# Three PSUM banks in turn, and logits relative to the first tap's

## The reference

```
k = conv(x, w1, 7x7, dilation 2, pad 6) + b1      # 256 -> 128 channels
k = conv(k, w2, 1x1) + b2                         # 128 -> 49 logits a pixel
attn = softmax(k over the 49)
x = sum over the 49 taps of shifted(x) * attn
```

## Time and profile before

| what | us |
|---|---|
| median of 3 runs (1031.37 to 1032.67) | 1032.48 |
| the profiled execution | 1033.16 |
| its span, first to last instruction | 1031.4 |
| PE busy | 870.8 (84%) |
| PE weight loads busy | 815.1 (79%) |
| DVE busy | 670.4 (65%) |
| ACT busy | 378.2 (37%) |
| POOL busy | 321.5 (31%) |
| mean granted TensorE clock, of full speed | 0.94 |

### The profile page before, as it was taken

The page is one execution under the profiler, slowest core; times in us unless marked ns, Lnnn a source line. Parts: engine busy times, 40 slices in busy tenths (PEclk is TensorE's granted clock), DMA queues, the critical chain, the costliest instruction groups (busy, mean ns, idle before and its releaser), DMA issues.

```text
span 1031.4 us, 13805 instructions
## 1 busy us (share of the span) xinstructions
PE 870.8 (84%) x5084; PEld 815.1 (79%) x5084; DVE 670.4 (65%) x913; ACT 378.2 (37%) x647; POOL 321.5 (31%) x257
## 2 busy tenths in 40 slices
PE   5548969898998998999899899899667649969992
PEld 5548969898998998999899799899656537758882
DVE  1765677567778678676667767855544455139994
ACT  1222211243333433344344243333333466133267
POOL 2536455263255245227224524422200000004000
PEclk9999989999999999999899999999867869989997
DMA  9600224966775794885577576464687977000099
GB/s 287 211 0 1 42 53 104 204 176 149 166 194 133 172 202 114 207 178 163 156 173 180 146 174 151 124 188 109 177 206 194 209 269 296 1 1 1 26 388 401
DMA packets 261851, 163.11 MB, mean 158 GB/s; under 512 B 203817, under 2 KB 244762, under 8 KB 259226
## 3 DMA queue, kind: packets, MB, share of 16 engines
q1 hardware_dynamic: 261786, 162.24, 58.7%
HBM read 103.41 MB, written 53.97 MB: 153 GB/s over the span
## 4 chain that ended last, share of the span: by engine, by line
PE 49%; DVE 26%; DMA 8%; issue 7%; ACT 5%; POOL 2%; SPq 2%; DVEq 0%; ACTq 0%; POOLq 0%
PE ps L782 13%; PE ps L783 13%; PE ps L784 13%; DVE logit L1156 4%; DVE logit L1147 4%; DVE whole L1063 3%; PE ps L848 3%; DVE xbuf L1083 3%; DMA dn<-logit 3%; PE ps L888 3%; PE ps L805 2%; ACT y L774 2%; PE ps L858 2%; DMA out<-y 2%; DVE wsum L1036 2%
## 5 line engine op out<-in xcount | busy, mean ns | idle before, releaser
L782 PE MATMUL ps<-w_hi,ring 128*128 128x350 f32 x832 | 282.5, 340 | 12.1 <-DVE logit L1147 11.4
L784 PE MATMUL ps<-w_hi,ring 128*128 128x350 f32 x832 | 273.9, 329 | 0.0
L783 PE MATMUL ps<-w_lo,ring 128*128 128x350 f32 x832 | 273.5, 329 | 0.0
L551 POOL TENSOR_TENSOR ring<-whole,ring 128x576 fp32r<-128x576 f32 x112 | 168.2, 1503 | 263.5 <-ACT ring L618 263.5
L782 PEld LDWEIGHTS ps<-w_hi,ring 128*128 128x128 f32 x832 | 162.2, 195 | 13.4 <-issue 12.8
L783 PEld LDWEIGHTS ps<-w_lo,ring 128*128 128x128 f32 x832 | 161.8, 194 | 0.5
L784 PEld LDWEIGHTS ps<-w_hi,ring 128*128 128x128 f32 x832 | 160.9, 193 | 0.0
L618 ACT ACTIVATE ring<-whole 128x576 fp32r<-128x576 f32 x112 | 86.4, 775 | 142.3 <-DVE whole L1063 100.2
L618 ACT ACTIVATE band_hi<-ps 128x320 fp32r<-128x320 f32 (+1 forms) x128 | 53.6, 419 | 190.9 <-PE ps L848 190.7
L782 PE MATMUL ps<-band_hi,xT_hi 128*128 128x224 f32 (+2 forms) x320 | 99.2, 310 | 17.0 <-DVE x_lo L1000 10.0
L1000 DVE TENSOR_TENSOR band_lo<-ps,band_hi 128x320 fp32r<-128x320 f32 (+1 forms) x128 | 58.8, 459 | 72.5 <-ACT band_hi L618 72.4
(11 more groups left out here) (127 smaller groups left out, 1435.2 us busy)
## 6 DMA issues: line engine op xcount, KB each, us to landing
xq<-in_x SPq DMA_DIRECT2D x128, 256.0 KB, 4.0
raw<-bands SPq DMA_DIRECT2D x32, 768.0 KB, 5.5
xbuf<-in_x SPq DMA_DIRECT2D x16, 1024.0 KB, 8.5
x_dram<-x SPq DMA_DIRECT2D x32, 512.0 KB, 2.8
x1in<-x_dram SPq DMA_DIRECT2D x8, 2048.0 KB, 17.0
out<-y SPq DMA_DIRECT2D x16, 1024.0 KB, 4.5
bands<-wide SPq DMA_DIRECT2D x32, 398.0 KB, 5.5
w1raw<-in_L_conv_w SPq DMA_DIRECT2D x2, 3136.0 KB, 12.6
```

The source lines that it names most:

```text
L551: pool.tensor_tensor(split(k, 1), positions(whole[:, k % TBUFS, :], 0, 2), split(k, 0).bitcast(F32), ALU.subtract).then_inc(sig_lo_done, 1)
L782: pe.matmul(dst, l_hi, r_hi_, start=first, stop=False, **kw)
L783: pe.matmul(dst, l_hi, r_lo_, start=False, stop=False, **kw)
L784: return pe.matmul(dst, l_lo, r_hi_, start=False, stop=last, **kw)
```

## The change: what it does

- **48 columns.** `KP` is 48. The filter and the bias of tap 0 are subtracted from those of the other 48 (`w2T`, `b2row`), so the logits are relative to tap 0's, whose own is 0. The softmax takes the maximum with 0 and writes its negative as the entry of tap 0. All convolution matmuls have 336 columns instead of 350.
- **Combination.** The bias is laid out as 480 columns once and enters with the first step. ACT takes the HALF1 product out of its bank (`half_product`); DVE adds MHALF to it and subtracts it (`C_EVEN`, `C_ODD`), and four steps read only SBUF. 15 DVE steps a pair instead of 18, at other places of the half.
- **Softmax.** Normalising and masking are one pass over the probabilities instead of two, with a small product ahead of it.
- **Banks.** `band_T`, `x_T` and `proj` take the banks 5, 6 and 7 in turn (`turns`, `take_bank`), each when the one three turns before has been read. The prologue's filter groups take four banks in turn (`psW`).
- **x_lo.** `x1_lo` is made by POOL from `x1` (SBUF) instead of by DVE from PSUM, as long as the convolution runs; in halves 16 to 19 DVE makes it, from `x1` too. The first unit of a half image waits for the copy alone.
- **c_of** is four instructions of 576 columns, each of which waits for the one before.
- **Order.** The spill is issued before the x1 store. In each engine's half the steps are placed anew: `softmax_top` in part 4, `softmax_end` and `y_out(tail, 1)` in part 7, `proj(tail, 1)` in part 5, `proj(image, 0)` in part 14 after unit 6, ACT's `x_out` ahead of `sig_hi`, DVE's signal of a half's last slot ahead of the last `xT` and `band_lo`.

```diff
-KP = KK + 1
+KP = KK - 1
+        psW = [ps[:, 3, :], ps[:, 4, :], ps[:, 7, :], ps[:, 6, :]]
+        turns = []
+        for q in range(HALVES):
+            conv, first, image, tail, coming, soft = schedule(q)
+            for kind, of, i in (("band", image, 0), ("x", image, 0), ("band", image, 1), ("band", image, 2),
+                                ("proj", tail, 1), ("x", image, 1), ("band", image, 3), ("band", image, 4),
+                                ("x", image, 2), ("band", image, 5), ("band", image, 6), ("x", image, 3),
+                                ("band", image, 7), ("proj", image, 0)):
+                if of is not None:
+                    turns.append((kind, of, i))
+        turn_of = {t: n for n, t in enumerate(turns)}
+        def turn_bank(kind, g, i):
+            return ps[:, 5 + turn_of[kind, g, i] % 3, :]
+        def take_bank(eng, kind, g, i):
+            n = turn_of[kind, g, i]
+            if n >= 3:
+                before, gb, ib = turns[n - 3]
+                if before == "band":
+                    eng.wait_ge(band_lo_done, NT * gb + ib + 1)
+                elif before == "x":
+                    eng.wait_ge(xT_lo_done, 4 * gb + ib + 1)
+                else:
+                    eng.wait_ge(y1_done, 2 * gb + ib + 1)
+            return turn_bank(kind, g, i)
...
             def c_of(i):
                 pool.wait_ge(b_done, i + 1)
-                n = 2 * (SH * XC // 2)
-                pool.tensor_tensor(xflat(i)[:, 0:n], xflat(i)[:, 4:n + 4], xflat(i)[:, 0:n], ALU.subtract).then_inc(c_done, 1)
+                n = SH * XC // 4
+                for j in range(4):
+                    if j:
+                        pool.wait_ge(c_done, 4 * i + j)
+                    a, b = (xflat(i)[:, o + n * j:o + n * (j + 1)] for o in (0, 4))
+                    pool.tensor_tensor(a, b, a, ALU.subtract).then_inc(c_done, 1)
...
+            def x_lo(g, h):
+                for cb in range(CB):
+                    pool.wait_ge(x1_done, 4 * g + 2 * h + cb + 1)
+                    pool.tensor_tensor(x1_lo[:, cb, :], x1[:, cb, :], x1_hi[:, cb, :].bitcast(F32), ALU.subtract
+                                       ).then_inc(x1_lo_done, 1)
             def slot(k):
+                q, c = divmod(k, SLOTS)
+                conv, first, image, tail, coming, soft = schedule(q)
+                if c == 1 and tail is not None:
+                    x_lo(tail, 1)
+                if c == 6 and image is not None:
+                    x_lo(image, 0)
+                if k + RING - 1 < NCHUNK:
                     signal(k + RING - 1)
+                if k + RING - 2 < NCHUNK:
                     sig_lo(k + RING - 2)
...
+            def half_product(s):
+                act.wait_ge(chunk_done, chunk_at(s, HALF1, CB - 1) + 1)
+                act.wait_ge(comb_done, comb(s, C_EVEN - 1))
+                act.activation(me[:, :], ps[:, BANKS[HALF1], 0:BANK], ACT.Copy, scale=16 / 9).then_inc(half_done, 1)
...
@@ half(q) of DVE @@
+                for part in range(2 * SLOTS):
+                    if part == 0 and soft is not None:
+                        combine(soft, C_INF)
+                    if part == 0 and tail is not None:
+                        y_out(tail, 0)
+                    if conv is not None:
+                        todo = ({10: (C_ONE,), 12: range(C_SUM, C_EVEN)} if q % 2 == 0 else
+                                {6: range(C_EVEN, C_ZERO), 12: (C_ZERO,)})
+                        for i in todo.get(part, ()):
+                            combine(conv, i)
+                    if part == 2 and conv is None and tail is not None:
+                        x_lo(tail, 1)
+                    if part == 4 and soft is not None:
+                        softmax_top(soft)
+                    if image is not None:
+                        if part in (1, 3, 5):
+                            bandlo(image, part // 2)
+                        if part in (2, 6, 9):
+                            xT(image, (2, 6, 9).index(part))
+                        if part in (7, 8):
+                            bandlo(image, part - 4)
+                        if part in (10, 11):
+                            bandlo(image, part - 5)
+                    if part == 7 and soft is not None:
+                        softmax_end(soft)
+                    if part == 7 and tail is not None:
+                        y_out(tail, 1)
+                    if part == 12 and conv is None and image is not None:
+                        x_lo(image, 0)
+                    if part % 2 and conv is not None:
+                        signal_slot(first + part // 2)
+                if image is not None:
+                    xT(image, 3)
+                    bandlo(image, 7)
```

More of the change, by code:

```diff
@@ L521, in _ @@
                 pool.memset(t, 1.0).then_inc(consts, 1)
+            pool.memset(bias[:, :], 0.0).then_inc(consts, 1)
             for c0, c1 in ((0, 2 * PAD), (2 * PAD + W, XC)):
@@ L588, in slot @@
                         pads(i)
+            signal(1)
+            sig_lo(0)
+            signal(2)
+            sig_lo(1)
+            sig_lo(2)
             for i in range(5):
                 filter_lo(i)
-            for k in range(1 - RING, 0):
-                slot(k)
+            c_of(0)
             for i in range(5, CB * len(WHOLES)):
@@ L646, in _ @@
                         whole_hi(len(WHOLES) * cb + j)
-                if (cb, v) == (0, 5):
-                    for k in range(RING - 2):
-                        sig_hi(k)
+                if (cb, v) == (0, 4):
+                    sig_hi(RING - 3)
                 if v == 6:
@@ L718, in half @@
-                    if c == 6 and image is not None:
-                        xT(image, 3)
-                        bandhi(image, 7)
-                        yhalf(image, 0)
+                    if part % 2 and conv is not None and first + part // 2 + RING - 2 < NCHUNK:
+                        sig_hi(first + part // 2 + RING - 2)
+                if image is not None:
+                    xT(image, 3)
+                    bandhi(image, 7)
+                    yhalf(image, 0)
             def prepare():
@@ L897, in half @@
                             band_T(image, part // 2)
-                        if part in (1, 5, 8):
-                            x_T(image, part // 3)
-                        if part == 4:
-                            unit(image, 0)
-                        if part in (6, 7):
-                            band_T(image, part - 3)
-                            unit(image, part - 5)
+                        if part == 1:
+                            x_T(image, 0)
+                    if part == 5 and tail is not None:
+                        proj(tail, 1)
+                    if image is not None:
+                        if part == 5:
+                            unit(image, 0)
+                            x_T(image, 1)
+                        if part == 6:
+                            band_T(image, 3)
+                            unit(image, 1)
+                        if part == 7:
+                            band_T(image, 4)
+                        if part == 8:
+                            unit(image, 2)
+                            x_T(image, 2)
                         if part == 9:
```

249 lines of the change are left out of this document (112 added, 137 removed).

## The result

| | us |
|---|---|
| before, median of 4 runs (1031.37 to 1032.67) | 1032.45 |
| changed, median of 4 runs (1080.79 to 1088.79) | 1085.17 |
| ratio, 95% interval | 1.051, 1.0485 to 1.0536 |
| its profiled execution, span | 1086.1, 1084.3 |
| DVE, POOL, PE busy (before 670.4, 321.5, 870.8) | 641.6, 435.1, 884.5 |

The change is slower by 5.1%. 1003.6 (951 to 1046) was predicted.

A forecast was written before the change was run, and what follows sets the result against it. It took PE's stream with holes from waits on DVE, and handover chains in prologue and tail, as the bound: 1033.2 - 19 - 1.8 + 0.9 + 8.5 - 2.5 - 15 = 1004.3, 1003.6 us beside the median, range 951 to 1046.

The forecast's parts named there:

- Columns: Convolution matmuls: 336 columns in place of 350 save 5.8 ns each, 14.6 us over 2,496 matmuls, 1.8 a pair.
- first pair: First pair of halves: only the saved columns count, -1.8 us.
- prologue: Filter making before the convolution: four banks and earlier steps start the convolution at 65 instead of 84, -19 us.
- Old waits: PE's waits on DVE in a pair, 5.5 us for the band bank and 1.0 for xT_lo, all go: -6.5.
- y waits: The bank turn makes band_T(4) wait for y_out(tail,1): 3.3 us in an odd half, 2.5 in an even half.
- proj's wait for x_lo: Odd half's end: PE's proj(image,0) waits 4.2 us for POOL's x_lo behind the differences, bounds 0 to 9.6.
- rival B: Odd half's end: DVE's signal block and POOL's work exclude each other, a 9.6 us wait; 1046 us, chance 0.20.
- The pair: Five steady pairs: savings against new waits make +1.7 us each, 86.7 a pair, +8.5 in sum.
- the eighth: Eighth pair, with no block to prepare: -1.8 - 6.5 + 5.8 = -2.5 us.
- second pair: Second pair, without tail projection: columns -1.8, small waits -1.5, wait for x_lo +4.2, together +0.9 us.
- The tail: Images without convolution, 733 to 829.4: shorter waits for band_lo and x_lo, -15 us, bounds -6 and -22.
- A: Steady pairs: the new waits do not come, 3 us of wait a pair in place of 10; 960 us, chance 0.30.

The follow-up runs named there:

- e4: Changed kernel with x_T(1) taking its bank ahead of proj(tail, 1) in the turn of the three banks: 1055.53 us.
- e2: Changed kernel with DVE's last signal block of a half behind the last xT_lo and band_lo again: 1078.46 us.
- e5: Changed kernel with the three order edits of e1, e2 and e4 together: 1015.68 us.
- e7: e5 plus e6's later differences and DVE's y_out(tail, 0), xT_lo(1), xT_lo(2) and odd half's first signal block placed anew: 1009.77 us.
- e8: e5 with the 13 y loads issued behind the last image's first-half x1 store, not ahead of it: 1011.29 us.
- e10: Changed kernel with bank turn mended, DVE's block last, e7's DVE steps, x_lo made by DVE, y loads one half earlier: 994.25 us.
- e13: e10 with x_lo made by POOL, the first half image's ahead of slot 5's signal: 1007.15 us.
- e16: e10 with the 13 y loads back where the changed kernel has them: 989.60 us.
- e1: Changed kernel with POOL's x_lo(image, 0) in slot 5, ahead of the next block's differences: 1062.25 us.
- e6: Changed kernel with POOL's differences of even blocks (c_of) two slots later, in slot 0 of the next even half: 1079.49 us.
- e12: Changed kernel with the differences (c_of) as one POOL instruction of 2,304 columns in place of four of 576: 1087.76 us.
- e14: e10 with the 13 y loads behind the last image's first-half x1 store: 987.40 us.
- e15: e10 with the 13 y loads in half 18 behind the first xq load: 990.74 us.

## Why the prediction was wrong

- **Columns, first pair, prologue.** The mechanism was right, w_lo behind the sums and the signal block with three groups left (42 records from 56.04). -20.8 predicted up to the second pair, -21.2 measured; first convolution matmul 65 and 65.23. 5.8 ns a matmul predicted, 6 to 7 measured (154 against 161). Right.
- **Old waits.** band_lo's are gone from the pairs. Right; but the 6.5 us of the one pair that was read stood for all, and over the five they are 5.6 in the mean (23.2 and 4.8).
- **y waits.** 3.3 and 2.5 predicted, 2.93 and 2.93 measured. Right. e4: taking them away gives 29.6 us.
- **proj's wait for x_lo: the step that failed.** It had four pieces at 4.8 and two x_lo at 2.1 behind sig_lo, as if POOL ran alone (alone they would be 4.6 and 2.5); they took 7.9 and 3.6, and the wait was 8.2 (40.8 over five) in place of 4.2. POOL's busy time says the same: 34.2 us a pair before, 52.0 after, where the forecast's prices make some 44. This is rival B, which had 9.6, 1.6 of low clock, and a chance of only 0.20. I held it back because no row of before showed that the two meet. But the forecast had itself put both into parts 12 to 14, and the earlier trace rows had the price: to add durations measured alone was the error. B was wrong in form: it is not block against differences one after the other; each instruction waits for the one under way, and with pieces they alternate. Hence e2, which parted block and differences, gained little.
- **The clock.** The forecast put no price on it behind its new waits, though B did. It is 12.5 us over five pairs in the matmuls of 320 and more columns, and some 21 with projections, transposes and narrow units (the +12.0 above without the -9.0 of columns).
- **The pair.** 86.7 predicted, 96.4 measured: 4.0 of the 9.7 are x_lo, 0.5 xT_lo, 0.9 the old waits that were not there to be saved, 4.2 the clock (2.5 in the wide matmuls). Over six pairs with the eighth (-2.5 predicted, +11.5 measured) that is 61.8 of the 81.8 us between 1004.3 and 1086.1. 8.4 of the eighth's 14.0 is the sixth wait for x_lo, by the place of the cut. For the same reason the second pair's +1.2 against the +0.9 predicted is luck: the forecast's 4.2 of x_lo fall behind that cut.
- **The tail.** -15 predicted, +4.6 measured: 19.6. The prediction let image 15's gain be lost to the y loads and counted the gains ahead of it. The gains came: waits for band_lo fell from 14.8 to 4.3 us, and the 10.0 for x_lo before the first units became 2.4 for ACT's copy. It had not counted that the turn makes PE wait for y here too (10.7 us from 778 to 882), nor 3.2 more for xT_lo and 2.7 for xq, so that all waits there fall only from 36.5 to 33.7; and PE's instructions between the waits take 7 us more, with ten matmuls more in the stretch and a granted clock of 0.73 in place of 0.77. The runs with the turn mended (e4, e5, e7, e8, e10, e13 to e16) all stay at 300 to 310 us from the last convolution matmul to the end, where before had 301.1 and the changed kernel 306.2. That the y loads hold up whatever they stand ahead of is shown; that the tail would be 15 shorter without them was not tried.
- **A** ("the new waits do not come") had 0.30 and nothing of it came.
- **Small readings.** The eight filter sums end at 57.6, not 57.2. B's "1.6 us at the lower level" is what was lost: the level itself lasted from 153.53 to 156.9.

## What to carry to other kernels

Where two engines exclude each other, a step moved from the fuller one to the emptier one is priced by what it meets there, and by whose chain it enters: x_lo on POOL was 1.35 us instead of 1.1, and cost 12.9 us over the kernel even at the last place tried. When banks or slots are used in turn, list for each take what must have been read, and where that reader stands in its own queue; one exchange in such a list was worth 29.6 us. After a wait is removed, price the next thing in the same queue before summing: e4 took away 42.8 us of waits for y and 23.2 came back as waits for xT_lo, e1 took away 49.2 for x_lo and 29.2 came back. And price the clock behind each wait that is left.

## What the runs showed of the hardware

- A two-input SBUF step on DVE that meets a POOL instruction waits for the end of that one only, and its recorded duration holds the wait: 3.66 with 1.22 to go and 2.56 alone (e6), 4.37 with 3.76 to go and 0.75 alone (e12), both within 0.15. Splitting POOL's instruction bounds what DVE pays to one piece (1.15 alone), and leaves POOL to pay DVE's whole steps (x_lo 5.31 for two in e2).
- 13 loads of 256 KB took 8.4 to 9.7 us to issue, and the transfer behind them on the queue landed 10 to 12 us after its issue (x1 store 10.8 changed, 11.0 e16, 9.9 e14; xq load 11.6 e15). The next x1 store of the changed kernel, with nothing ahead of it, landed 2.8 us after its issue.
- In the changed kernel 19 of 20 waits of PE of 2.9 to 8.5 us between 130 and 760 us are followed by matmuls at the lower clock level (durations 0.63 and 0.48 us, 0.28 apart). The one at 473.92, with the same 2.93 us of wait as at 428.59, is not; what sets it apart was not tried.
